# Macaron block on one core: seven more items in the last feed-forward chunk, and the first output projection's contexts loaded early into own buffers

## What is computed

```python
def _L0_ffn_ref(x, k0, k1, k2, s0, s1, s2):
    h = jnp.concatenate([x, -x], axis=-1)
    h = s0 * _conn_dense(k0, h)          # weights +1 or -1
    h = jax.nn.relu(h) * 2
    h = s1 * _conn_dense(k1, h)
    h = jax.nn.relu(h) * 2
    return s2 * _conn_dense(k2, h)
...
scores = jnp.einsum('bhqd,bhkd->bhqk', q, k) / jnp.sqrt(jnp.float32(DK))
scores = jnp.where(causal[None, None], jnp.float32(-1000000000.0), scores)
attn = jax.nn.softmax(scores, axis=-1)
ctx = jnp.einsum('bhqk,bhkd->bhqd', attn, v)
...
return ctx @ w_o.T + b_o
...
x = x + 0.5 * _L0_ffn_ref(_layernorm(x), ...)
x = x + _L0_attn_ref(_layernorm(x), ...)
x = x + 0.5 * _L0_ffn_ref(_layernorm(x), ...)
```

## Time and profile before

| | |
|---|---|
| time, three runs | 1571.55 us median (1568.6 to 1572.48) |
| the profiled execution's own time | 1570.29 us |
| its span, first to last instruction | 1568.6 us |
| part A, up to the first score | 459.7 us |
| part B, up to the second network's first matmul | about 747 us |
| granted clock of TensorE, mean | 0.996 |

### The profile page before, as it was taken

One profiled execution on the slowest core, in us unless ns is written; L12 is line 12 of the kernel. 1 busy time (PEld: TensorE's weight loads), 2 busy tenths in 40 slices (PEclk: granted clock), 3 DMA queues, 4 the chain that ended last, 5 costly groups with the idle time before them and its releaser, 6 DMA issues.

```text
span 1568.6 us, 35438 instructions
## 1 busy us (share of the span) xinstructions
PE 1539.0 (98%) x14112; PEld 725.5 (46%) x14112; DVE 1124.6 (72%) x1616; ACT 840.4 (54%) x1702; POOL 189.8 (12%) x514
## 2 busy tenths in 40 slices
PE   6999999999989999999999999999999999999998
PEld 3555555555433333343334333333333555555554
DVE  6535543554568999989988999998896667666552
ACT  3223322332148888888888888888886222222221
POOL 4300000000011122121122121112111000000000
PEclk9999999999989999999999999999999999999999
DMA  5122023202032222211222211222212221211210
GB/s 171 28 68 57 10 67 94 67 13 67 1 111 60 70 62 69 52 43 53 70 69 62 69 38 49 61 69 63 70 69 82 71 77 70 72 52 61 80 27 14
DMA packets 146227, 96.39 MB, mean 61 GB/s; under 512 B 106544, under 2 KB 125616, under 8 KB 146096
## 3 DMA queue, kind: packets, MB, share of 16 engines
q1 hardware_dynamic: 146096, 94.54, 21.6%
HBM read 49.15 MB, written 37.75 MB: 55 GB/s over the span
## 4 chain that ended last, share of the span: by engine, by line
PE 95%; DVE 2%; ACT 1%; SPq 1%; DMA 0%; issue 0%; DVEq 0%
PE ffn_mm L434 28%; PE ffn_mm L1266 18%; PE ffn_mm L1286 16%; PE ffn_mm L420 7%; PE ffn_acc L450 7%; PE ffn_acc L626 6%; PE ffn_tr L626 5%; PE ffn_mm L721 3%; PE ffn_acc L733 2%; PE ffn_acc L546 2%; DVE m_part L647 1%; PE ffn_tr L404 1%; ACT probs L1238 1%; PE ffn_tr L632 1%; PE ffn_acc L632 0%
## 5 line engine op out<-in xcount | busy, mean ns | idle before, releaser
L1238 ACT ACTIVATE probs<-ffn_mm 128x512 f32<-128x512 f32 (+3 forms) x1280 | 597.3, 545 | 122.1 <-PE ffn_mm L1266 116.3
L647 DVE TENSOR_REDUCE m_part<-ffn_acc 128x2 f32<-128x1024 f32 (+2 forms) x345 | 367.2, 1064 | 33.9 <-PE ffn_acc L626 29.1
L1266 PE MATMUL ffn_mm<-qk 128*32 128x512 f16 (+7 forms) x5120 | 387.9, 355 | 2.5 <-ACT probs L1238 1.8
L434 PE MATMUL ffn_mm<-ffn_h1h,w 128*128 128x512 f16 x1024 | 388.2, 379 | 0.0
L434 PE MATMUL ffn_mm<-ffn_h1l,w 128*128 128x512 f16 x1024 | 388.1, 379 | 0.0
L647 DVE TENSOR_REDUCE m_part<-ffn_tr 128x2 f32<-128x1024 f32 (+3 forms) x295 | 311.1, 1054 | 40.0 <-PE ffn_tr L626 24.7
L1286 PE MATMUL ffn_mm<-probs,v 128*32 128x512 f32 (+3 forms) x2560 | 305.5, 535 | 0.1
L500 ACT ACTIVATE ffn_h2h<-ffn_mm 128x512 f16<-128x512 f32 x128 | 76.4, 597 | 292.5 <-PE ffn_mm L434 291.1
L1266 PEld LDWEIGHTS ffn_mm<-qk 66*32 66x32 f16 (+1 forms) x5120 | 135.3, 94 | 210.2 <-ACT probs L1238 115.6
L511 DVE SCALAR_TENSOR_TENSOR ffn_h2l<-ffn_mm,ffn_h2h 128x512 f16<-128x512 f32 x128 | 85.7, 686 | 170.8 <-ACT ffn_h2h L500 170.8
L434 PEld LDWEIGHTS ffn_mm<-ffn_h1l,w 128*128 128x128 f16 x1024 | 100.2, 98 | 118.8
...
## 6 DMA issues: line engine op xcount, KB each, us to landing
qk<-qk_scr SPq DMA_DIRECT2D x256, 64.0 KB, 2.7
...
```

The costliest lines, as they stand in the source:

```text
L434: ins = nc.tensor.matmul(f.mm[:, m % 4, :], w1[:, kt, m * P:(m + 1) * P], part[:, kt, :], start=(kt == 0 and part is f.h1h), stop=(kt == H ...
L647: nc.vector.tensor_reduce(m_part[u][:, t, :, r], s_ps[slot][:, :, 0:w], AX.X, ALU.max).then_inc(sb.s_done, 1)
L1238: nc.scalar.activation(probs[:, g % P_SLOTS, j, c0:CH], st_ps[bank(k)][:, c0:CH], ACT.Exp, scale=scale_now).then_inc(se.exp_done, 1)
L1266: ins = nc.tensor.matmul(st_ps[bank(k)][c:c + 32, c0:CH], k_part(pair % 2, h, rows, slice(kb * P + c, kb * P + c + 32)), q_part(pair % 2, ...
```

## The change

1. All 26 items of `AHEAD` run in part A's last chunk: 20 in `pe_l1` (two or three a row, by the table `L1_FILLS`), 3 in `pe_l2`, 3 in the last `pe_qk`. A table gives each its slot, now alternating. The seven items at the head of part B are gone. The wait for the last value evictions moves to the first item behind pair 0's second step.
2. SP stores the rows of turn 1 in part A, ahead of the last two chunks' stores.
3. ScalarE runs one tiny exponential (`exp_first`) ahead of the last two value evictions, so that its table is loaded there.
4. The first projection's contexts have buffers of their own, the hidden layer's `h1h` and `h1l`, which part B doesn't use. SP loads them in pairs 9 to 12, two DMAs behind each pair's loads. GpSimd adds the two halves: the weights in pair 13, step 14, the numerators in pair 14, step 14.
5. VectorE inverts a quarter of the weights ahead of its last item, and the rest behind it; it adds nothing for chunk 0.
6. The first output projection is cut into its four tiles, behind scores (13, 2), (14, 0), (14, 2) and (15, 0).
7. The load that stands in pair 15 is now that of the second chunk's contexts, and the later load with its wait ahead of SP's stores is gone.

```diff
-        def load_ctx(sp, b, i):
+        ctx_first, wgt_first = (buf[:, :, :].rearrange("p m n -> p (m n)").bitcast(F32).rearrange("p (a t n) -> p a t n", a=2, t=DT)
+                                for buf in (fc.h1h, fc.h1l))
+
+        def load_ctx(sp, b, i, to=(ctx_in, wgt_in), done=sc.ctx_in, parts=range(2 * DT)):
...
+        def pool_first_sum(dst, done):
+
+            nc.gpsimd.wait_ge(sc.first_in, 128)
+            nc.gpsimd.tensor_tensor(dst[:, 0, :, :], dst[:, 0, :, :], dst[:, 1, :, :], ALU.add).then_inc(done, 1)
+
+        FIRST_PARTS = ((0, slice(0, 256)), (0, slice(256, CH)), (1, slice(0, CH)))
+
+        def dve_first_inverse(kt, cols):
+
+            wait(nc.vector, sc.wgt_sum, 1)
+            nc.vector.reciprocal(wgt_first[:, 0, kt, cols], wgt_first[:, 0, kt, cols]).then_inc(sc.wgt_part, 1)
...
-        OUT_PROJ_STEP = STEPS - 5
+        OUT_PROJ_AT = {(STEPS - 7, 2): 0, (STEPS - 6, 0): 1, (STEPS - 6, 2): 2, (STEPS - 5, 0): 3}
+        FIRST_SUM_PAIR, FIRST_SUM_STEP = ALL_PAIRS - 3, STEPS - 6
+        FIRST_LOAD_PAIRS = range(PAIRS + 1, PAIRS + 5)
...
-        EARLY = [0] * 15 + [1] * 3 + [0]
-        EARLY_T2 = 4
-        slots = EARLY + [n % 2 for n in range(len(EARLY), len(AHEAD))]
+        L1_FILLS = ((7,), (2, 5, 7), (2, 5, 7), (3, 7), (2, 5, 7), (2, 5, 7), (2, 5, 7), (2, 7))
+        L2_FILLS, QK_FILLS = 3, 3
+        slots = [1] + [0, 1, 0] + [1, 0, 1] + [1, 0] + [1, 0, 1] + [0, 1, 0] + [1, 0, 1] + [0, 0] + [0, 0, 0] + [0, 1, 0]
...
+                for i in range(2):
+                    sp_rows(sp, 0, i, AHEAD.index(("turn", i)))
                 store(1, QCH - 2)
                 store(1, QCH - 1)
...
                 act_qk(c, range(2 * DT))
+                nc.scalar.activation(exp_first[:, :], exp_scale[:, :], ACT.Exp)
                 act_v(c)
...
+                    if n == tr_after_turn:
+                        wait(pe, se.x2_t, NCH - 1)
+                    if n == acc_after_v:
+                        wait(pe, se.v_ev, (NCH - 1) * 2)
+                    pe_early(n)
...
                                     if last:
-                                        load_ctx(sp, 0, 0)
+                                        load_ctx(sp, 0, 1)
                                     else:
                                         load_pair(sp, 1 - pair % 2, pair + 1)
+                                    if pair in FIRST_LOAD_PAIRS:
+                                        for sem in ctx_st:
+                                            sp.wait_ge(sem, 8 * PAIRS * QCH)
+                                        load_ctx(sp, 0, 0, (ctx_first, wgt_first), sc.first_in, [FIRST_LOAD_PAIRS.index(pair)])
                             if j == PV_POINTS[s % STEPS] and g in ends:
                                 n = ends.index(g)
-                                if last and n == len(ends) - 2:
-                                    wait(sp, sc.ctx_n, 1)
-                                    load_ctx(sp, 0, 1)
                                 store(n // QCH, n, n % QCH)
...
                 for g in range(ALL_STEPS):
                     pair, s = divmod(g, STEPS)
+                    if pair == FIRST_SUM_PAIR and s == FIRST_SUM_STEP:
+                        pool_first_sum(wgt_first, sc.wgt_sum)
+                    if pair == FIRST_SUM_PAIR + 1 and s == FIRST_SUM_STEP:
+                        pool_first_sum(ctx_first, sc.ctx_sum)
...
-                for n in range(len(EARLY), len(AHEAD)):
-                    if n == len(EARLY):
-                        pe.wait_ge(sa.v_ev, NCH * 2)
-                    pe_early(n)
                 pe.wait_ge(sa.qk_lo, NCH * 4)
...
+                        if pair == ALL_PAIRS - 1 and (s, j) in OUT_PROJ_AT:
+                            wait(pe, se.s_done, ALL_PAIRS * S_USES)
+                            pe_out_proj(pe, 0, lambda j: None, [OUT_PROJ_AT[s, j]])
...
+                def normalize_first():
+
+                    for kt, cols in FIRST_PARTS[1:]:
+                        dve_first_inverse(kt, cols)
+                    wait(dve, se.wgt_part, len(FIRST_PARTS))
+                    wait(dve, se.ctx_sum, 1)
+                    nc.vector.tensor_tensor(proj_in[:, :, :], ctx_first[:, 0, :, :], wgt_first[:, 0, :, :], ALU.mult).then_inc(se.ctx_n, 1)
```

87 lines of the change are left out of this document (47 added, 40 removed).

## The result

| | median | runs |
|---|---|---|
| before | 1570.17 us | 5, 1568.6 to 1572.48 |
| changed | 1562.92 us | 5, 1560.37 to 1563.65 |
| ratio | 0.9953, 95% interval 0.9941 to 0.9965 | |

A forecast was written before the change was run, and what follows sets the result against it. TensorE was taken as the bound, busy for 98% of the span. 8.5 us at the seam and 2.4 at the end off 1571.55 gave 1560.6 us; range 1557.5 to 1567, with 1558 to 1562.5 at 0.68.

The forecast's parts named there:

- The items: Part A's last chunk: seven more items cost 2.8 us, 2.55 us of waits go, so the value projection ends at 452.9.
- rival (d): Part A's last chunk: dense fills stall TensorE; at 0.75 us an item the kernel takes 1580 us; chance 0.03.
- The table load: Ahead of the last value evictions: 1.28 us from about 449.9, while TensorE is in the projection; first exponential at 453.6.
- The wait for the stores: Pair 0, exponential k = 12: waits 1.5 us, from 459.1, for part A's stores, in at 460.5.
- the 1.70 us wait at 1202.72 cost no clock: Transposes behind pair 15: this wait of before, without a clock fall, was held against a fall at pair 0's start.
- pair 1's pace: Pair 0, k = 12 to 17: takes 3.5 us as in pair 1, so k = 17 comes at 464.1.
- the seam: Where parts A and B meet: 8.5 us gained by k = 17, of which the first exponential's earlier start is 6.8.
- rival (a): Pair 0's start: the clock falls all the same, costing 4 to 6.5 us, time 1564.6 to 1567.1; chance 0.14.
- Rival (e): Pair 0: the wait for part A's stores is longer, to 464 or so, time 1564; chance 0.05.
- Costs that I put at nothing: Pairs 9 to 14: added context DMAs, about 1.3 us of SP, and two GpSimd additions, 2.8 us each, cost nothing.
- The end: End of pair 15: earlier contexts and the projection in four pieces start the transposes 2.4 us earlier.
- The slack of 1.05 us: Pair 15's last three steps: TensorE needs 1.73 us a step, ScalarE 2.08; the pieces use the difference, the block did not.

The follow-up runs named there:

- late_table: early_ctx without the tiny exponential ahead of the last value evictions, so the table load lies behind them again: 1561.03 us, ratio 0.9941.
- end_only: The kernel before with only the change's end part (early contexts, GpSimd's sums, projection in four pieces): 1568.92 us, ratio 0.9995.
- hold_clock: early_ctx with five additional matmuls of 512 columns on TensorE in pair 0's first three steps: 1559.11 us, ratio 0.9926.
- warm_wait: The changed kernel with 12 additional matmuls on TensorE ahead of score k = 15, while ScalarE waits for the stores: 1563.5 us, ratio 0.9957.
- own_seam: Changed kernel without its end part, last chunk's queries and keys in other memory, SyncE's store wait behind pair 1's loads: 1559.91 us, ratio 0.9932.
- early_ctx: Changed kernel, last chunk's queries and keys in other memory, SyncE's store wait behind pair 1's loads, contexts loaded in pairs 8 to 11: ratio 0.9921.
- loads_only: seam_only with the eight context loads into h1h and h1l in pairs 9 to 12, which nothing reads: 1564.11 us, ratio 0.996.
- seam_only: The changed kernel with its end part undone (contexts, sums and output projection as before): 1563.54 us, ratio 0.9963.

## Why the prediction came out as it did

**The items, right.** 2.8 us for seven items less 2.55 us of waits was to bring the first score at 452.9; it started at 452.28, 0.5 us better with the start taken off, which was not traced further. The items' waits come to 0.5 us from 384 to 480, where rival (d) needed over 10; it is dead.

**The table load, right.** It ran from 449.64, where it was put, and the first exponential started at 452.92 (forecast 453.6). late_table shows that its place was worth more than its own 1.28 us: once the stores no longer hold k = 12, 3.1 us by the ratios.

**The wait for the stores, mis-sized.** The low half was done at 450.40 (forecast 450.6), but the stores were in by 461.8, 11.4 us later, not 9.8. ScalarE got to k = 12 at 458.5 rather than 459.1. So the wait was 3.36 us, not 1.5. SyncE issued the twelve stores within 0.4 us of where before's stood. Before's last store landed at 460.39, 0.4 us behind the first quiet moment that the prediction took. The other 1.2 us are in the last store. The view of the DMA queues from 457 to 461.5 us has its time from issue to landing as the last figure, 4.0 us before and 5.4 after, and for the changed kernel a packet of a second queue, q8, which before has not got there:

```profile
v_scr<-v_pad SPq DMA_DIRECT2D x1, 256.0 KB, 4.0
```

```profile
q8 instruction: 1, 0.02, 1.3%
...
v_scr<-v_pad SPq DMA_DIRECT2D x1, 256.0 KB, 5.4
```

So it is the tail of the transfers. The changed kernel's windows of half a microsecond, to be held against the earlier trace rows, where the share fell to 0.02 at 460.0:

```profile
460.00:460.50 0.50, 0.00 (x0) 0.00 (x0) 0.50 (x2) 0.00 (x0) 0.00 (x0) 1.00 0.58 140
460.50:461.00 0.50, 0.00 (x0) 0.00 (x0) 0.50 (x1) 0.00 (x0) 0.00 (x0) 1.00 0.08 13
461.00:461.50 0.50, 0.00 (x0) 0.00 (x0) 0.47 (x1) 0.00 (x0) 0.00 (x0) 1.00 0.06 13
```

Few engines are at work there, and the wait is for the last one. 9.8 us was one execution's figure and was used as a constant. The traces have a likely reason. The q8 packet is one of the 16 KB instruction packets that count in pair 12; it moved from 459.20 to 460.15, among the last store's. Before has its packet at 465.87, behind all stores: TensorE's first score is 7.4 us earlier in the changed kernel, and this packet 6.7. In the ten executions where it started 2.2 to 3.0 us ahead of the last store's landing, that store took 5.3 to 5.8 us. In before and end_only, which have none there, it took 4.0, in late_table, where it came 0.5 us ahead, 4.6, and in hold_clock, where it came behind, 4.4. No run moved the packet by itself, so that it is the cause is not shown.

**The clock, the wrong rival preferred.** "Against it: ... the 1.70 us wait at 1202.72 cost no clock" was the step that failed. The sum let pair 1's pace hold from k = 12 on; it took 5.51 us to k = 17, not 3.5. warm_wait shows the cause: the idle TensorE. own_seam shows that the very wait which the prediction held against it, 1.70 us ahead of the transposes, can be followed by a fall, and in early_ctx and loads_only it fell with no wait over 0.7 us ahead of it. Together with the wait the seam gave 5.2 us of the 8.5 at k = 17, and 3.9 by the end of pair 0. That rival (a) had 0.14 was too little, since all five executions have a mean clock under 1.000; its price, 4 to 6.5 us, was too high: 2.7, and 1.6 in seam_only. Rival (e), a longer wait for the stores, came too, by a third of its size (461.8 against 460.5, where it had 464).

**The added loads, not free.** "Costs that I put at nothing" counted SyncE's 1.3 us and named the store behind them. It did not ask who else uses the DMA engines. In the profiled executions of the seven kernels with the loads in pairs 9 to 12 right behind a pair's loads the price was 0.46, 0.46, 1.37, 1.55, 1.75 and 1.84 us, and 3.78 in end_only, where the clock fell behind the stop. GpSimd's sums were free: 2.37 us each, and they ran behind a turn's columns and not ahead of them.

**The end, 1.4 of 2.4.** The wait of 1.70 us went as forecast. The slack of 1.05 us, which was to give the rest, was not there. It took ScalarE for the bound of the three steps at 2.08 us a step. But TensorE was idle for 0.94 us besides that wait before and for 0.98 us after, so nothing of it was used, and its busy time rose by 0.26: 1.70 - 0.04 - 0.26 = 1.40. A piece took 1.06 us (1181.03 to 1182.09), not 0.86. The contexts were ready 0.35 us before their place. That part of the end was right.

**The total.** 5.2 - 1.3 + 1.4 less 0.46 for pair 12 gives 4.8 us between the two profiled executions; the other 1.9 of their 6.7 is the start (0.13), 0.5 in pair 7 and 0.9 in pair 14, where before's execution waited longer for loads, and 0.4 in pair 13 that was not traced. The ratio gives 7.4. So what was forecast, 10.9, came to less than half by the mechanisms that it was built on, and the difference between executions made up part of it: that is luck. 1562.92 lies outside the band of 1558 to 1562.5 that had 0.68, and the range held since its upper end was set by the case of a falling clock, which is the case that came.
